# Flash attention over a long context on one core: row maxima turned without negation, a context remainder made one addition later

## What is computed

```
q = (x @ Wq + bq).reshape(B, N, 16, 32)
k = (y @ Wk + bk).reshape(B, M, 16, 32)
v = (y @ Wv + bv).reshape(B, M, 16, 32)
scores = einsum('bnhd,bmhd->bhnm', q, k) * scale
attn = softmax(scores, axis=-1)
out = einsum('bhnm,bmhd->bnhd', attn, v)
```

## Time and profile before

| | us |
|---|---|
| median of 3 runs | 3046.11 |
| lowest and highest run | 3045.59, 3048.97 |
| the profiled execution's own time | 3049.87 |
| its span from first to last instruction | 3048.0 |
| PE busy | 2937.2 |
| DVE busy | 2250.0 |
| POOL busy | 2022.4 |
| ACT busy | 1682.5 |

### The profile page before, as it was taken

How to read it: one execution, slowest core, us unless ns; L and a number is a source line. 1 busy time by engine, 2 the same in 40 slices (tenths; PEclk the granted TensorE clock), 3 DMA queues, 4 the chain that set the end, 5 groups by cost and what they waited for, 6 DMA issues and landing times.

```text
span 3048.0 us, 39906 instructions
## 1 busy us (share of the span) xinstructions
PE 2937.2 (96%) x14712; PEld 1804.6 (59%) x14712; DVE 2250.0 (74%) x3368; ACT 1682.5 (55%) x2920; POOL 2022.4 (66%) x745
## 2 busy tenths in 40 slices
PE   7999999999999999999999999999999887899999
PEld 4666666666666666666666666666534333344477
DVE  7777777777777777777777777777746899986653
ACT  1566666666666666666666666666641555321021
POOL 1699999999999998999999999999950000000000
PEclk9999999999999999999999999999999989999999
DMA  6534444454434445443444434443450112214100
GB/s 167 136 81 101 111 110 91 96 118 98 101 88 117 97 122 129 106 114 89 101 101 117 95 91 112 110 102 80 89 194 12 52 54 97 82 56 167 69 14 18
DMA packets 108886, 296.10 MB, mean 97 GB/s; under 512 B 23762, under 2 KB 28882, under 8 KB 99122
## 3 DMA queue, kind: packets, MB, share of 16 engines
q1 hardware_dynamic: 99044, 226.71, 26.6%
q0 software_dynamic: 9072, 66.06, 11.5%
q10 hardware_dynamic: 576, 0.79, 0.1%
HBM read 114.46 MB, written 8.06 MB: 40 GB/s over the span
## 4 chain that ended last, share of the span: by engine, by line
PE 86%; DVE 10%; ACT 1%; issue 1%; DMA 1%; POOL 0%; SPq 0%; ACTq 0%; DVEq 0%; POOLq 0%
PE ps L1828 16%; PE ps L1867 15%; PE ps L1854 14%; PE ps L1781 9%; PE ps L1812 9%; PE ps L1805 8%; PE ps L2077 4%; PE ps L2041 4%; DVE pm L1053 3%; PE ps L2057 3%; PE ps L1884 2%; DVE bx L1315 1%; PE ps L1836 1%; PE ps L2069 1%; ACT V L1523 1%
## 5 line engine op out<-in xcount | busy, mean ns | idle before, releaser
L1053 DVE TENSOR_REDUCE pm<-ps 128x1 f32<-128x512 f32 x2048 | 1408.2, 691 | 523.4 <-PE ps L1828 450.7
L1537 ACT ACTIVATE pf<-ps 128x512 f32<-128x512 f32 x2048 | 1218.8, 600 | 695.5 <-PE ps L1854 610.8
L900 POOL TENSOR_TENSOR psum<-psum,pf 128x2048 f32<-128x2048 f32 x317 | 1455.6, 4592 | 25.2 <-ACT pf L1537 9.0
L1828 PE MATMUL ps<-ks,qs 96*128 96x512 f32 x2048 | 847.8, 414 | 25.1 <-DVE pm L1053 19.8
L1854 PE MATMUL ps<-qs,ks 98*128 98x512 f32 x2048 | 814.2, 399 | 3.4 <-ACT pf L1537 3.3
L1828 PEld LDWEIGHTS ps<-ks,qs 96*128 96x128 f32 x2048 | 387.1, 189 | 291.9 <-issue 201.5
L1867 PE MATMUL ps<-pf,V 128*32 128x512 f32 x4096 | 496.0, 602 | 0.0
L1854 PEld LDWEIGHTS ps<-qs,ks 98*128 98x128 f32 x2048 | 391.2, 191 | 50.1 <-ACT pf L1537 13.0
L915 POOL PARTITION_ALL_REDUCE qstat<-qstat x2 | 0.7, 367 | 605.5 <-DVE qstat L1351 605.5
L900 POOL TENSOR_TENSOR psum<-pf 128x2048 f32<-128x2048 f32 x64 | 303.2, 4738 | 53.5 <-ACT pf L1537 53.5
L1805 PE MATMUL ps<-cTh,Wkg 128*128 128x512 f32 x732 | 292.9, 400 | 2.7
(11 more groups left out here) (224 smaller groups left out, 3029.6 us busy)
## 6 DMA issues: line engine op xcount, KB each, us to landing
ks<-KH SPq DMA_DIRECT2D x512, 128.0 KB, 3.1
psum<-pf POOLq DMA_DIRECT2D x63, 1024.0 KB, 7.8
ks<-KL SPq DMA_DIRECT2D x256, 128.0 KB, 3.1
cT<-in_ctxT SPq DMA_DIRECT2D x32, 768.0 KB, 4.7
Wkg<-wk_rows SPq DMA_DIRECT2D x61, 384.0 KB, 5.5
BC<-bc_rows SPq DMA_DIRECT2D x32, 512.0 KB, 4.8
ring<-in_ffn_w SPq DMA_DIRECT2D x16, 1024.0 KB, 7.8
wA<-in_W_fcT SPq DMA_DIRECT2D x4, 1024.0 KB, 10.1
```

The source lines that it names most:

```text
L900: pool.tensor_tensor(acc, before, pf[:, tile % P_SLOTS, :], ALU.add).then_inc(s_sum, 1)
L1053: dve.tensor_reduce(pm[:, n // BLK, n % BLK:n % BLK + 1], src, AX.X, ALU.max).then_inc(s_wfree, 1)
L1537: act.activation(pf[:, tile % P_SLOTS, j * NTOK:(j + 1) * NTOK], ps[:, S_BANK + u % S_BANKS, :], ACT.Exp, scale=SCALE).then_inc(s_exp, 1)
L1828: last = pe.matmul(dst, qs[0:3 * HD, h, t * P:(t + 1) * P], ks[0:3 * HD, keys_of(of, j), i * 512:(i + 1) * 512], start=True, stop=True)
```

## The change

The negation is gone: `nm` and its semaphore are dropped, PE turns `mn` itself once `s_fin` says that it is there, and the rows beside the keys are set to minus one. DVE no longer waits for its own reduction to `mn`, so `pm` gets two buffers, which the groups take in turn. In the table, the first half of the context remainder stands ahead of addition 1 where it stood ahead of addition 0.

```diff
-LOW_AT = {0: 0, 4: 1}
+LOW_AT = {1: 0, 4: 1}
...
-        pm = sb("pm", [P, HG * NT, BLK + 1], c=att)
+        pm = sb("pm", [P, 2, HG * NT, BLK + 1], c=att)
...
-                pool.memset(ks[3 * HD:SROWS, g * HG:(g + 1) * HG, :].bitcast(F32), 1.0).then_inc(s_ones, 1)
+                pool.memset(ks[3 * HD:SROWS, g * HG:(g + 1) * HG, :].bitcast(F32), -1.0).then_inc(s_ones, 1)
...
-                dve.tensor_reduce(mn[:], pm[:], AX.X, ALU.max).then_inc(s_fin, 1)
-                dve.wait_ge(s_fin, of + 1)
-                dve.tensor_scalar(nm[:], mn[:], -1.0, None, ALU.mult).then_inc(s_nm, 1)
+                dve.tensor_reduce(mn[:], pm[:, of % 2], AX.X, ALU.max).then_inc(s_fin, 1)
...
-                    pe.wait_ge(s_nm, x[1] + 1)
-                    last = pe.transpose(dst[0:HG * NT, 0:P], nm[:], ident[:])
+                    pe.wait_ge(s_fin, x[1] + 1)
+                    last = pe.transpose(dst[0:HG * NT, 0:P], mn[:], ident[:])
```

More of the change, by code:

```diff
@@ L349, in emit @@
         s_dm = sem("s_dm")
-        s_nm = sem("s_nm")
         s_mrow = [sem(f"s_mrow{g}") for g in range(NG)]
@@ L450, in emit @@
         dt_ = sb("dt_", [P, NTOK], c=att)
-        pm = sb("pm", [P, HG * NT, BLK + 1], c=att)
+        pm = sb("pm", [P, 2, HG * NT, BLK + 1], c=att)
         mn = sb("mn", [P, HG * NT], c=att)
         dm = sb("dm", [P, HG * NT], c=att)
-        nm = sb("nm", [P, HG * NT], c=att)
         al = sb("al", [P, 2, HG * NT], c=att)
@@ L881, in keep_max @@
                     if of // NG == NCH - 1 and g == NG - 1:
-                        pool.memset(pm[:, :, BLK], LOWEST).then_inc(s_seed, 1)
+                        pool.memset(pm[:, (of + 1) % 2, :, BLK], LOWEST).then_inc(s_seed, 1)
                     else:
                         n = (of + 1) % NG
-                        pool.tensor_copy(pm[:, :, BLK], m_run[:, n * HG * NT:(n + 1) * HG * NT]).then_inc(s_seed, 1)
+                        pool.tensor_copy(pm[:, (of + 1) % 2, :, BLK], m_run[:, n * HG * NT:(n + 1) * HG * NT]).then_inc(s_seed, 1)
             pool.wait_ge(s_lowest, 1)
@@ L987, in _ @@
             dve.wait_ge(s_small, 32)
-            dve.memset(pm[:, :, BLK], LOWEST)
+            dve.memset(pm[:, 0, :, BLK], LOWEST)
             dve.memset(m_run[:], LOWEST).then_inc(s_lowest, 1)
@@ L1052, in empty @@
                     of, n = divmod(x[1], HG * A_UNITS)
-                    dve.tensor_reduce(pm[:, n // BLK, n % BLK:n % BLK + 1], src, AX.X, ALU.max
+                    dve.tensor_reduce(pm[:, of % 2, n // BLK, n % BLK:n % BLK + 1], src, AX.X, ALU.max
                                       ).then_inc(s_wfree, 1)
```

## The result

The changed kernel takes **3104.6 us** (median of 5 runs, 3102.67 to 3113.25). Beside it on the same chip the kernel before took 3047.21 us (5 runs, 3045.59 to 3051.56). The ratio is 1.019, 95% interval 1.0179 to 1.0201: slower by 57 us. The forecast was 3052.7 with a range to 3067. The direction was right, though a forecast of +6.6 us is hardly more than the 6 us that the prediction itself counted as no change. The size was not: the term that the prediction called the one that decides, PE's longer wait at place 2, was sized nearly three times too small, and the clock, which follows from it, four times.

What follows compares the result with a forecast made beforehand. PE, busy for 96% of the span, was taken as the bound. Terms -16.6 + 13.5 + 1.2 + 8.5 = +6.6 us gave 3056.5 on the profiled execution, 3052.7 us for the median; range 3032 to 3067.

Steps and rivals of the forecast that it cites:

- the term that the prediction called the one that decides: At place 2 of a chunk, the key stack lands 0.9 us later per group: +13.5 us over 15 groups.
- place 1: The 15 groups at position 1 of a chunk: PE no longer loses time to the negation, -16.6 us.
- place 2, waiting: Groups at position 2 of a chunk: PE waits longer for the key stack, +13.5 us, and +1.2 for one group.
- place 2, the clock: PE's longer waits at position 2 of a chunk halve its clock in five groups, 1.7 us each: +8.5 us.
- The negation: DVE's `nm` removed: groups at place 1 of a chunk fall to 33.56 us, 16.6 us gained in all.
- POOL's delay: Moving the remainder makes POOL 1.27 us later at place 1; tail transfer issued 11.2 us into the next group.
- The half remainder: At place 1, ready at about 413.9 against 408.0, costing nothing; a rival had it too late for the key products, 2%.
- the upper bound: Key stack at place 2 at most 1.9 us later, if it still waits out the whole tail transfer.
- rival of the full shift: Tail transfer delays the stack at place 2 by all 1.9 us, ten groups lose the clock: +30, 3076 us; 12%.
- the lower bound: Key stack at place 2 at least 0.6 us later, if the DMA engines stay full from the weights on.
- small term of +1.2 us: Group 1248.49 at place 2, hardly waiting today after a long predecessor, comes to wait like the others: +1.2 us.
- The first rival: Key stack at place 2 does not notice the later tail transfer; only the 16.6 us gain remains, 3029.5 us; 15%.

Runs made afterwards that it cites:

- e2_remainder_only: Kernel before with the half remainder moved ahead of addition 1 and the negation kept: 3071.77 us, ratio 1.0073.
- e1_negation_only: Changed kernel with the remainder put back ahead of addition 0, so only the negation is gone: 3053.85 us, ratio 1.001.
- e6_after_two_steps: Changed kernel with raw products for the maxima two steps later and keep_max behind POOL's fourth addition: 3069.84 us, ratio 1.0062.
- e3_small_tail: Changed kernel with POOL's tail transfer cut to an eighth, 256 of 2048 columns: 3013.49 us, ratio 0.9883.
- e10_tail_copies: Changed kernel with the tail transfer as a plain copy in place of an addition: 3024.59 us, ratio 0.9916.
- e8_keep_fourth_only: Kernel without the negation, remainder ahead of addition 0, keep_max behind POOL's fourth addition instead of the third: 3040.95 us, ratio 0.9971.
- e7_tail_in_halves: Changed kernel with the tail transfer issued as two halves of 1024 columns each: 3379.87 us, ratio 1.1082.

## Why the prediction was wrong

| term | predicted | measured |
|---|---|---|
| place 1 | -16.6 | -16.9 |
| place 2, waiting | +13.5 and +1.2 | +39.7 |
| place 2, the clock | +8.5 | +33.1 |
| sum | +6.6 | +55.9 |

**The negation** was right, in mechanism and size: a group of place 1 takes 33.56 us, the number written down, and the long group is gone.

**POOL's delay** was right: second addition 16.98 us into the group ("about 17"), tail transfer at 11.1 ("11.2"). The half remainder was in time. The run e2_remainder_only bears out a side of it that the sum did not need: with the negation still there, the same delay would have cost place 1 about 21 us.

**The step that failed** is "At least 0.6 us ... if they stay full ... At most 1.9 us: all of the shift ... I take 0.9, near the lower end, since the engines are full and the total work is the same". The shift was 1.9 us and the stack's end moved by 2.6 to 2.7, beyond the upper bound. The bounds took it that the engines do the same work in whatever order it comes. Three things in that were wrong.

*Whose packets share the engines.* A packet is the piece of a transfer that the trace records for one DMA engine: 8 KB for the tail, 4 KB for the stack, 3 KB for the weights. DMA queues over the stretch in which the tail transfer moves, first before (442.0 to 448.0), then changed (725.2 to 732.6): packets, MB, share. q0 is POOL's queue, q1 is SP's.

```profile
q0 software_dynamic: 113, 0.93, 74.2%
q1 hardware_dynamic: 125, 0.38, 17.6%
```

```profile
q0 software_dynamic: 114, 0.84, 66.7%
q1 hardware_dynamic: 158, 0.46, 30.1%
```

Before, the 0.38 MB of SP are the key weights, all of them. No packet of the stack moved until the tail transfer was through (16.9 us into the group for both); then all 12 stack transfers followed alone in 7.1 us. In the changed kernel the weights are through before the tail's first packet (12.6 for both), and it is the stack that runs beside the tail. By the medians of place 2, an engine moves on average 8.0 packets of the weights beside its 8 of the tail before, and 8.4 of the stack's 24 beside them after. A packet of the tail takes 0.66 us before and 0.75 after, one of the stack about 0.27 to 0.29. So the stack starts 3.5 us earlier and advances slowly, the tail's own packets take 8.7 us from first to last instead of 6.2, and two thirds of the stack are still to come when they end, at 21.35 where it was 16.91. The slow issues of SP fall in the stretch in which the tail moves, in both kernels.

*The engine time.* Windows of both kernels, in each the whole stretch from the weights to the product, then the part with the tail transfer, and the rest of the stack alone; the last two numbers are the DMA share and GB/s:

```profile
441.13:455.53 14.40, 13.86 (x86) 8.80 (x84) 10.70 (x17) 8.76 (x16) 14.24 (x5) 1.00 0.90 210
441.90:448.10 6.20, 6.20 (x44) 4.53 (x37) 4.71 (x8) 3.62 (x7) 6.12 (x3) 1.00 0.98 227
448.10:454.90 6.80, 6.80 (x41) 4.00 (x39) 4.80 (x8) 4.13 (x8) 6.72 (x2) 1.00 0.96 229
```

```profile
721.84:738.84 17.00, 13.96 (x86) 8.90 (x84) 10.44 (x16) 8.73 (x16) 16.41 (x6) 0.96 0.85 178
725.20:732.60 7.40, 7.40 (x50) 5.07 (x49) 5.42 (x8) 4.78 (x9) 7.32 (x2) 1.00 0.97 176
732.70:738.30 5.60, 2.99 (x13) 2.09 (x11) 2.97 (x5) 2.39 (x4) 5.52 (x2) 0.93 0.84 195
```

Both whole stretches move the same 3.02 MB (14.40 x 210, 17.00 x 178). Before, that took 14.40 x 0.90 = 13.0 us of packet time on 16 engines, and after 17.00 x 0.85 = 14.5: **1.5 us more for the same bytes**. The share adds up the times of packets, so it says how long they are under way and not how much they carry. At 0.97 the engines carry 176 GB/s with tail and stack together; with tail and weights it was 227 at 0.98. A part of that drop is the mix, since weight packets are the fastest of the three; the rest is that packets of each kind take longer.

*The gaps.* The other 1.1 us (17.00 - 14.5 idle against 14.40 - 13.0) are time without packets. The rest of the stack ran at a share of 0.96 before, 12 transfers at 0.59 us each, and at 0.84 in the changed kernel. There SP, held up until then, starts an issue every 0.64 us, and this probably sets the pace; no run tests it.

"The total work is the same" held for bytes, not for time.

The prediction's rival of the full shift had the mechanism in half a sentence ("the stack has 12 transfers to issue while the tail moves"), and gave it 12%. The row that could have raised it was in the trace of the kernel before: in its group of 431.13 three of SP's issues are slow, while in a group of place 0, where the tail is issued at 5.6, it is as a rule one:

```profile
442.64 0.52 SPq L657 DMA_DIRECT2D ks<-KH  x1
443.20 1.47 SPq L657 DMA_DIRECT2D ks<-KL  x1
444.71 3.49 SPq L657 DMA_DIRECT2D ks<-KH  x2
448.24 0.68 SPq L657 DMA_DIRECT2D ks<-KL  x1
```

Three slow issues cost 1.47 + 3.49 - 3 x 0.59 = 3.2 us there. I had read the first and the last row of this queue and not those between.

Of the Trainium skill's rule cited for the lower bound (DMA: Bandwidth & Descriptors, "Queues, rings and completion order": the queues that have work take turns, packet by packet), the packets agree: 8.0 of the weights, or 8.4 of the stack, to 8 of the tail on an engine. The prediction took from it only that the stack advances. A turn packet by packet, with tail packets of 0.75 us, also means that the stack gets a third of its packets through in all of the tail's 8.7 us. And the rule had nothing to say for the kernel before, where the stack lay behind the weights in its own queue and did not advance at all.

**The clock** term was missized twice over. The falls were in 14 of the 15 groups where five were taken; this comes from the first error, since PE idled for 3.0 to 4.2 us a group and not for 1.9. In e1_negation_only, where 13 of the 15 groups idle for 1.2 to 2.4 us, the clock fell in six groups. So five was a fair guess for the wait that was forecast. And twelve of the falls lasted 6.8 us and cost 2.5 us each, against 1.7 taken from one fall of 3.4 us; the two falls of 3.4 us cost 1.5 each. In all 2 x 1.5 + 12 x 2.5 = 33. That a fall can last 6.8 us is a thing of its own: in e6_after_two_steps, with 1.6 to 2.6 us idle, five groups have no fall, six one of 3.4 and four one of 6.8 (36.8 us busy, 3.1 more than without). The length of the wait alone does not say which.

The small term of +1.2 us is worked out from no row; by the rows, a group that came to wait like the others would add 0.8.

**The first rival**, that the stack does not notice, had "the same bytes through engines that were full" against it. That was the right verdict from a wrong reason. e1_negation_only shows that even 0.7 us of shift is passed on in full.

**Open** remain three things. Why an issue of SP takes up to 2.7 us while POOL's transfer is under way: size and kind of the transfer matter, as e3_small_tail and e10_tail_copies show, but what SP waits for was not seen. Why packets take longer when tail and stack run together. And why, for a tail anywhere between 8.65 and 9.24 us, the weights are through only at 17.0, so that the stack starts at 16.8 and the product is 0.9 us late: in e8_keep_fourth_only the first packet of the weights starts at 14.15, in the kernel before at 11.55.

## What to carry to other kernels

A share of 0.97 in the DMA engines says that packets are under way, not whose they are nor what they carry: read the packets and MB of each queue and the GB/s beside it, and ask which transfers will share the engines in the new order, before bounding a shift. When a change moves one queue's transfer across another's, read every issue of both queues in that stretch; slow issues in the kernel before are the warning. And a stall taken from the engine that bounds the kernel is worth only what the next fixed deadline leaves of it: here the same edit gave nothing alone, cost 57 us with a second edit, and saved 26 once the deadline was moved along with it.

## What the runs showed of the hardware

- While POOL's 1 MB adding transfer was under way beside the key stack (changed kernel, place 2), four to six of SP's 12 issues took 1.0 to 2.7 us each where one takes 0.59; with the transfer cut to 128 KB mostly one was slow (0.9 to 1.8). At place 0 of the kernel before, where the tail is nearly through, one in most groups is slow as well (up to 1.5 us).
- The two queues took turns: to 8 packets of the tail (8 KB each) an engine moved 8.0 of the weights (3 KB) in the kernel before and 8.4 of the stack (4 KB) in the changed one.
- A second POOL transfer behind a first was not issued until 3.9 to 7.6 us later, 0.6 to 1.2 us behind the first one's last packet (63 groups of e7_tail_in_halves).
- The same bytes written as a copy landed 4.9 us after the issue, as an addition 7.6 (medians of 63). At place 2, a packet of 8 KB took 0.39 us as a copy and 0.75 as an addition.
- With tail and stack at work the engines carried 176 GB/s at a share of 0.97, with tail and weights 227 at 0.98, with the stack alone 229 at 0.96.
- A `nm` of 128 by 16, 0.18 us long otherwise, took 1.8 us (median) where a POOL addition covered it, and ended with the addition within 0.04 us.
- After 3.0 to 4.2 us of idle time PE's clock was at half for 6.8 us in twelve groups, for 3.4 in two and not at all in one (changed kernel); after about 1.8 us, for 3.4.
